# A fused MoE, attention and MoE kernel: the first group's turn and transfers in another order, four projection tiles behind the last mix, and a re-cut second routing

## The chip, the cores and the metric

The kernel runs on one core of one Trainium2 chip. The metric is the device time of one execution in microseconds, given as the median of several runs. All inputs and the output lie in HBM; one launch computes everything.

## The reference, cut to what matters

```python
# _moe_forward: E=8 experts, top 2 per token, capacity C=1280, h=256, F=512
x = x + 0.5 * ffn(layernorm(x))        # first routing and experts
x = x + attention(layernorm(x))        # 4 batches x 1024 tokens, 16 heads of 16
x = x + 0.5 * ffn(layernorm(x))        # second routing and experts
# attention: scores = Q K^T / 4 + lambda * (tanh(Q) J) tanh(K)^T, causal softmax,
#            out = probs V, then out Wo^T + bo
# ffn: probs = softmax(x Wg); two best experts; rows over the capacity dropped;
#      gelu(a) * g per expert; the two results added with normalised gates
```

## The kernel before, in words

4096 tokens of 256 values are kept as 32 tiles of 128 tokens. The program has three blocks, each ended by a barrier of all engines: first routing and experts; projections and attention; second routing and experts (`route` is called with `tail` only there).

**Start of attention.** Attention works on 16 groups, each of four heads of one batch. Before the scores of a group, every row's maximum is bounded by a pass of 48 products ("units", `max_unit` on TensorE, `seen` on VectorE). Then VectorE takes the maximum over the parts (`top_of`), TensorE turns it (`turn`), ScalarE negates it and its queue stores it as a further row of the queries (`negate`, `row`); the first score of the group waits for that row (`row_in`). The list `EVENTS` sets the order of units and turns, and TensorE, VectorE and ScalarE walk through the same list: before, each turn stands LAG = 4 units behind its group's last unit. The first 12 units of group 1 and the projections of the third half batch are mixed into this list ahead of the first scores (`first_events`). The banks for the products are lent out in the order of the list, so a unit waits until VectorE has read an earlier one.

The data of the first two halves come from `project`: `pack[0]` to `pack[3]` (high and low parts of queries and keys, 2 MB each) and the values. They go to HBM in `packs` and `values`, and come back as the tiles of a group (`load_queries_and_keys`, four transfers, 3 MB; `load_values`). The SP engine issues all of these from one queue, in program order. Group 0 gets its tiles directly. `pack[2]` and `pack[3]` hold other heads, which groups 2 and 3 need; `late_out` counts their arrival. The exponents (`wts`) are written to memory that a `pack` held.

**End of attention.** In the last group the output projection is computed tile by tile among the scores (`("o", t)`, one tile at each of 16 steps; `out_tile`, `add_out`), for tiles 0 to 15. The attended values of a half batch are divided by the softmax sums beforehand by GpSimd (`average`, two halves in each of the last three groups; `average_tail`). After the last mix, ScalarE stores the result, and the barrier follows.

**Second routing.** The other 16 tiles are projected in pairs (`pair`: eight matrix instructions, then `add_pair` and `pair_stats` on VectorE). The first pairs rest on data averaged in attention, the last four pairs on values that must first be divided (`average` in `route`): the reciprocals of the sums are regrouped by head by a DMA (`by_head`) and spread over the 16 rows of a head by a product with `spreader`. Statistics give variances and deviations for the tiles of one of `PARTS`; `normalize` makes the rows, by ScalarE for the groups of four tiles in `BY_ACT` and by VectorE for the others; then come `transposes` (TensorE), `turned` (copies on ScalarE), `logits`, `taken`, `turn_back`, and on VectorE the choice of experts, slots and lists, behind which the first gather of rows and the experts start.

## Time and profile before

| | us |
|---|---|
| median of 3 runs | 1552.32 (1543.54 to 1553.25) |
| the profiled execution | 1552.77 |
| its span, from the first to the last instruction | 1551.0 |
| mean TensorE clock granted in it | 0.957 of full speed |

The profile is one execution. Its span is divided into busy time of the engines; an idle time has the engine or transfer behind it that ended it. The blocks lie at 0 to 420 us (first routing and experts), 425 to 1121 us (projections and attention) and 1125 to 1551 us.

### The profile page before, as it was taken

Reading aid. Unit: us, or ns where it says so; the run is one execution under the profiler, and the core shown is the slowest. Engines: PE = TensorE matmul, PEld = TensorE weight load, DVE = VectorE, ACT = ScalarE, POOL = GpSimd, SP = SyncE. Lnnn points to the kernel's source line nnn. Section 1 sums busy time; section 2 is a strip of 40 time slices with the busy share of each in tenths; the row PEclk is TensorE's granted clock in tenths of the full one; section 3 lists DMA queues with packets and bytes.
Section 4 is the critical chain, followed back from the end, with each engine's and each line's share of the span. In section 5 each row is a group of like instructions: output and inputs, shape, how many; then the busy total and the mean of one; then the engine's idle time right before and its main releaser. Section 6 shows DMA issues by size and latency. Waiting matters only on the chain. (4 is left out here: it accounts for less than half of the span.)

```text
span 1551.0 us, 25160 instructions
## 1 busy us (share of the span) xinstructions
PE 1437.4 (93%) x8872; PEld 1091.9 (70%) x8874; DVE 994.4 (64%) x2526; ACT 719.2 (46%) x1106; POOL 681.1 (44%) x654
## 2 busy tenths in 40 slices
PE   4699999999878899999999999999896999999998
PEld 3589889899866555555555555555565998898998
DVE  7756655555368576777777677886367566565554
ACT  5333333333263455555556565665473333333332
POOL 1365565664435442323333332225303655656644
PEclk9799999999989698989999999999987999999999
DMA  9454433442299866665656569562073444335432
GB/s 306 139 105 100 94 64 87 102 93 38 29 194 273 263 185 157 168 174 134 178 149 178 131 177 258 170 188 97 30 236 116 105 98 97 60 92 103 94 38 26
DMA packets 125509, 206.48 MB, mean 133 GB/s; under 512 B 24280, under 2 KB 86232, under 8 KB 122520
## 3 DMA queue, kind: packets, MB, share of 16 engines
q1 hardware_dynamic: 89032, 157.96, 36.3%
q0 software_dynamic: 30720, 38.46, 15.1%
q10 hardware_dynamic: 5648, 8.66, 1.9%
q8 instruction: 62, 1.02, 0.3%
q14 instruction: 47, 0.39, 0.1%
HBM read 123.22 MB, written 82.54 MB: 133 GB/s over the span
## 5 line engine op out<-in xcount | busy, mean ns | idle before, releaser
L2188 ACT ACTIVATE a_wts<-a_s_psum 128x1024 f32<-128x1024 f32 (+1 forms) x384 | 301.7, 810 | 218.3 <-PE a_s_psum L2323 216.3
L2060 DVE CUSTOM_DVE_ANT_0 a_m_psum<-a_m_psum,mask 128x256 f32<-128x256 f32 (+2 forms) x492 | 248.4, 519 | 140.7 <-PE a_m_psum L2289 130.4
L2289 PE MATMUL a_m_psum<-a_kp,a_qp 96*128 96x512 f32 (+1 forms) x735 | 275.9, 403 | 26.1 <-DVE a_parts L2060 17.4
L2289 PEld LDWEIGHTS a_m_psum<-a_kp,a_qp 96*128 96x128 f32 x735 | 142.4, 196 | 159.5 <-DVE a_parts L2060 81.0
L1997 POOL TENSOR_SCALAR_AFFINE_SELECT a_wts<-a_wts 128x512 f32<-128x512 f32 x128 | 78.2, 634 | 329.0 <-ACT a_wts L2188 328.8
L1032 ACT ACTIVATE e_act_a<-e_a_psum 128x512 f32<-128x512 f32 (+1 forms) x192 | 101.2, 527 | 259.4 <-PE e_a_psum L1111 259.4
L2323 PE MATMUL a_s_psum<-a_qp,a_kp 97*128 97x512 f32 (+2 forms) x768 | 213.8, 361 | 0.7 <-DMA a_qp<-stats 0.4
L949 DVE TENSOR_TENSOR e_hid<-e_act_a,e_g_psum 128x512 f32<-128x512 f32 (+1 forms) x192 | 114.7, 597 | 141.5 <-PE e_g_psum L1111 136.8
L243 POOL DMA_INDIRECT e_slots<-normalized,e_token x160 | 166.2, 1039 | 81.7 <-issue 47.5
L1130 PE MATMUL e_o_psum<-e_w_hi,e_h_hi 128*128 128x256 f32 x640 | 183.4, 287 | 0.0
L890 POOL DMA_INDIRECT out<-e_res,e_sum_row x80 | 126.5, 1582 | 126.5 <-ACT e_res L1044 113.1
L890 POOL DMA_INDIRECT sums<-e_res,e_sum_row x80 | 126.5, 1581 | 126.1 <-ACT e_res L1044 104.9
L1130 PE MATMUL e_o_psum<-e_w_hi,e_h_lo 128*128 128x256 f32 x640 | 181.0, 283 | 0.0
L1130 PE MATMUL e_o_psum<-e_w_lo,e_h_hi 128*128 128x256 f32 x640 | 181.0, 283 | 0.0
L2063 DVE TENSOR_REDUCE a_parts<-a_m_psum 128x1 f32<-128x512 f32 x243 | 159.2, 655 | 10.5 <-PE a_m_psum L2289 7.0
L2339 PE MATMUL a_o_psum<-a_wts,a_vg 128*17 128x512 f32 (+3 forms) x1536 | 159.8, 505 | 4.0 <-POOL a_wts L1997 2.7
L2323 PEld LDWEIGHTS a_s_psum<-a_qp,a_kp 97*128 97x128 f32 x768 | 136.5, 195 | 19.0 <-ACT a_wts L2188 4.7
L1044 ACT ACTIVATE e_res<-e_o_psum,e_gate 128x256 f32<-128x256 f32 x160 | 75.9, 475 | 147.7 <-PE e_o_psum L1130 147.7
L1111 PE MATMUL e_a_psum<-e_s_hi,e_w_hi 128*128 128x512 f32 (+1 forms) x384 | 139.3, 363 | 5.4 <-DVE e_s_lo L929 2.8
L1111 PE MATMUL e_a_psum<-e_s_lo,e_w_hi 128*128 128x512 f32 (+1 forms) x384 | 136.0, 354 | 0.0
L1111 PE MATMUL e_a_psum<-e_s_hi,e_w_lo 128*128 128x512 f32 (+1 forms) x384 | 136.0, 354 | 0.0
L1111 PE MATMUL e_g_psum<-e_s_hi,e_w_hi 128*128 128x512 f32 (+1 forms) x384 | 135.9, 354 | 0.0
(292 smaller groups left out, 2702.9 us busy)
## 6 DMA issues: line engine op xcount, KB each, us to landing
packs<-x_res SPq DMA_DIRECT2D x48, 512.0 KB, 5.9
e_w_raw<-in_W_in SPq DMA_DIRECT2D x16, 1024.0 KB, 6.6
a_qp<-packs SPq DMA_DIRECT2D x15, 1024.0 KB, 8.0
a_kp<-packs SPq DMA_DIRECT2D x15, 1024.0 KB, 14.0
e_w_raw<-in_W_out SPq DMA_DIRECT2D x16, 512.0 KB, 8.4
normalized<-r_xn SPq DMA_DIRECT2D x16, 512.0 KB, 4.4
attended<-a_o_sb ACTq DMA_DIRECT2D x32, 256.0 KB, 4.6
a_qp<-packs SPq DMA_DIRECT2D x15, 512.0 KB, 10.1
```

The costliest lines, as they stand in the source:

```text
L243: pool.indirect_dma_start(held["slots"][e % 2][:, j * ROW:(j + 1) * ROW], None, xn_dram, bass.IndirectOffsetOnAxis(ap=held["token"][:, at: ...
L890: nc.gpsimd.indirect_dma_start(sum_dram, bass.IndirectOffsetOnAxis(ap=sum_row[:, at:at + 1], axis=0), res[j][:], None, bounds_check=last_r ...
L949: nc.vector.tensor_tensor(hid[q][:, 0:n], act_a[q][:, 0:n], g_ps[q][:, 0:n], ALU.mult).then_inc(hid_done, 1)
L1032: nc.scalar.activation(act_a[q][:, 0:n], a_ps[q][:, 0:n], ACT.Gelu).then_inc(gelu_done, 1)
L1111: last = nc.tensor.matmul(bank[q][:, 0:n], w_in_at(w, k, half + f), s[:, k, c0:c0 + n], start=(z == 0), stop=(z == len(terms) - 1))
L1130: last = nc.tensor.matmul(o_ps[(u * ST + c0 // P + j) % 2][:, 0:D], s[:, k, j * P:(j + 1) * P], w_out_at(w, k), start=(z == 0), stop=(z == ...
L2060: nc.vector.tensor_tensor_reduce(products, products, c["mask"][:, QC - width:], 1.0, MASKED, ALU.add, ALU.max, top).then_inc(max_read, 1)
L2063: nc.vector.reduce_max(top, products, AX.X).then_inc(max_read, 1)
L2188: nc.scalar.activation(wts[(u * NS + s) % 2][:, j, 0:w], s_ps[q % 2][:, 0:w], ACT.Exp).then_inc(weighed, 1)
L2289: nc.tensor.matmul(m_ps[bank((n, h, z))][:, 0:stream], qp[n % NB][0:PACK, h, qt * P:(qt + 1) * P], kp[n % NB][0:PACK, h, first * P:first * ...
L2323: last = nc.tensor.matmul(s_ps[q % 2][:, col - lead:col + w], kp[u][:, j, kt * P:(kt + 1) * P], qp[u][:, j, at - lead:at + w], start=True, ...
L2339: last = nc.tensor.matmul(o_ps[j * HP:j * HP + HV, q0:q0 + w], vg[u][:, kt, j, :], wts[(u * NS + s) % 2][:, j, col:col + w], start=(kt == ...
```

## The change

It has two places. **At the start of attention** the turn of group 0 stands right behind its 48 units. The load of group 1 is issued ahead of `pack[2]`; the values of group 1 count on the semaphore of group 0's values, so its units wait for the four loads of queries and keys alone; the load of the next half of x follows; then `pack[3]` is sent, SP waits until it has arrived, and then sends `pack[2]`. The first exponent waits for the arrival of `pack[3]`. **At the end of attention** four more tiles (16 to 19) are projected behind the last mix, ahead of the barrier (`AFTER_LAST`); their averages are made one group earlier. The second routing has six pairs instead of eight. The regrouping of the reciprocals is done by VectorE (`place`) and a product over 128 rows in place of a DMA. `PARTS` is cut at tiles 20 and 24, and ScalarE normalizes groups 0 to 4 in another order; it also blanks `lgT_ps`.

```diff
-IN_ATTENTION = TAIL - SEQ // P
+U_TILES = 4
+IN_ATTENTION = TAIL - U_TILES
...
-    PARTS = [slice(0, U), slice(U, NT)] if r == 0 else [slice(0, U), slice(U, U + U // 2), slice(U + U // 2, NT)]
+    PARTS = [slice(0, U), slice(U, NT)] if r == 0 else [slice(0, IN_ATTENTION), slice(IN_ATTENTION, TAIL), slice(TAIL, NT)]
...
-        BY_ACT = (1, 2, 3) if r == 0 else (0, 1, 2, 3, 4, 5)
+        BY_ACT = (1, 2, 3) if r == 0 else (0, 1, 2, 3, 4)
...
-                sp.wait_ge(inverted, 1)
-                sp.dma_start(by_head[:].rearrange("h (l c) -> h l c", c=PER_LANE),
-                             divisors[:]).then_inc(heads_in, 16)
...
+            def place(z):
+                half = slice(z * LANES // 2, (z + 1) * LANES // 2)
+                nc.vector.tensor_tensor(by_lane[:, half, :], divisors[:].unsqueeze(1).to_broadcast([P, LANES // 2, PER_LANE]),
+                                        on_lane[:, half].unsqueeze(2).to_broadcast([P, LANES // 2, PER_LANE]), ALU.mult).then_inc(placed, 1)
+
             if tail:
                 variances(0)
+                link(nc.vector.reduce_sum(on_lane[:], c["ident"][:].rearrange("p (h l) -> p l h", l=LANES), AX.X))
+                deviations(0)
                 dve.wait_ge(sums_in, 16)
                 nc.vector.reciprocal(divisors[:], divisors[:]).then_inc(inverted, 1)
-                deviations(0)
-                nc.vector.memset(lgT_ps[:], 0.0).then_inc(blank, 1)
+                dve.wait_ge(inverted, 1)
+                place(0)
+                place(1)
                 add_pair(0)
+                average(0)
                 add_pair(1)
+                average(1)
                 pair_stats(0)
-                average(0)
-                average(1)
                 pair_stats(1)
+                dve.wait_ge(stats_done, TAIL - IN_ATTENTION)
+                variances(1)
                 add_pair(2)
+                deviations(1)
                 add_pair(3)
...
+                normalize(5)
+                pair_stats(4)
                 add_pair(5)
...
             roots(0)
+            if tail:
+                nc.scalar.activation(lgT_ps[:], c["mask"][:], ACT.Copy, scale=0.0).then_inc(blank, 1)
...
+                pair(2)
+                transposes(0)
+                pair(3)
                 pe.wait_ge(averaged, 2)
-                transposes(0)
+                transposes(1)
+                pair(4)
                 pair(5)
-                pair(6)
-                transposes(1)
-                pair(7)
                 logits(0)
...
-            if k >= LAG and (k - LAG) % PER_GROUP == PER_GROUP - 1:
+            if k == PER_GROUP - 1:
+                EVENTS.append((0, GH - 1, None))
+            if k >= PER_GROUP + LAG and (k - LAG) % PER_GROUP == PER_GROUP - 1:
                 EVENTS.append(((k - LAG) // PER_GROUP, GH - 1, None))
...
+        IN_LAST = IN_ATTENTION - U_HALF
+        AFTER_LAST = [("o", t) for t in range(IN_LAST, IN_ATTENTION)]
...
             load_values(sp, tiles[0], v_dram, 0, loaded[0])
-            load_values(sp, tiles[1], v_dram, 1, loaded[1])
-            proj["last_packs"](sp)
+            load_values(sp, tiles[1], v_dram, 1, loaded[0])
             next_half(FIRST_LATER + 1)
+            proj["last_packs"](sp, FIRST_LATER + 1)
+            sp.wait_ge(proj["late_out"], 4 * 16)
+            proj["last_packs"](sp, FIRST_LATER)
             packs_out(FIRST_LATER, 0)
...
-                        if g >= GROUPS - 3:
-                            for z in range(2):
-                                average((g - GROUPS + 3) * 2 + z)
+                        for i in {GROUPS - 3: (0, 1), GROUPS - 2: (2, 3, 4, 5)}.get(g, ()):
+                            average(i)
...
-                if m == GROUPS * PER_GROUP - 1:
+                if m in (PER_GROUP - 1, GROUPS * PER_GROUP - 1):
                     top_of(n)
...
+                        if (g, q) == (0, 0):
+                            act.wait_ge(proj["late_out"], 4 * 16)
                         nc.scalar.activation(wts[(u * NS + s) % 2][:, j, 0:w], s_ps[q % 2][:, 0:w], ACT.Exp).then_inc(weighed, 1)
...
-                    pe.wait_ge(loaded[n % NB], (n // NB * NL + (NL if n % NB else 1)) * 16)
+                    pe.wait_ge(loaded[n % NB], (n // NB * NL + (2, NL - 1, NL)[n % NB]) * 16)
...
             groups(body)
+            ahead(AFTER_LAST)
```

**The SP queue at the start of attention.** Before (rows on `q_pack` are `pack[2]` and `pack[3]`, four transfers each; `a_qp`, `a_kp` are group 1's tiles and then group 2's):

```order
L1214 DMA values<-q_vals 128x272 x8
L1206 DMA packs<-q_pack 64x4x512 x4
L1250 DMA a_qp<-packs 64x4096
L1250 DMA a_qp<-packs 32x4096
L1250 DMA a_kp<-packs 32x4096
L1250 DMA a_kp<-packs 64x4096
L1256 DMA a_vg<-values 128x544 x2
L1206 DMA packs<-q_pack 64x4x512 x4
L1198 DMA x_res<-sums 128x4x256
L1206 DMA packs<-x_res 64x4x512 x4
```

After:

```order
L1218 DMA values<-q_vals 128x272 x8
L1254 DMA a_qp<-packs 64x4096
L1254 DMA a_qp<-packs 32x4096
L1254 DMA a_kp<-packs 32x4096
L1254 DMA a_kp<-packs 64x4096
L1260 DMA a_vg<-values 128x544 x2
L1202 DMA x_res<-sums 128x4x256
L1210 DMA packs<-q_pack 64x4x512 x8
L1210 DMA packs<-x_res 64x4x512 x4
L1218 DMA values<-q_vals 128x272 x4
```

Group 1's loads and the load of x moved ahead of both packs.

**TensorE at the end of attention and in the second routing.** Before (the branches are the barrier; `r_list_psum`, `r_lg_psum` and `r_tp_psum` from `p_wo` are pairs):

```order
L2339 MATMUL a_o_psum<-a_wts,a_vg 17x256 x4
L2436 UNCONDITIONAL_BRANCH
L2417 UNCONDITIONAL_BRANCH
L295 MATMUL r_list_psum<-p_wo,p_mean_third 128x256 x4
L295 MATMUL r_lg_psum<-p_wo,p_mean_third 128x256 x4
L761 MATMUL r_tp_psum<-r_by_head,r_spreader 128x512 x2
L295 MATMUL r_tp_psum<-p_wo,p_mean_third 128x256 x8
L295 MATMUL r_list_psum<-p_wo,p_mean 128x256 x4
L722 MATMUL r_tp_psum<-ident,r_xn 128x128 x8
L295 MATMUL r_lg_psum<-p_wo,p_mean 128x256 x4
L295 MATMUL r_tp_psum<-p_wo,p_mean 128x256 x4
L722 MATMUL r_tp_psum<-ident,r_xn 128x128 x8
```

After:

```order
L2346 MATMUL a_o_psum<-a_wts,a_vg 17x256 x4
L295 MATMUL a_m_psum<-p_wo,p_mean_third 128x256 x8
L2444 UNCONDITIONAL_BRANCH
L2425 UNCONDITIONAL_BRANCH
L295 MATMUL r_list_psum<-p_wo,p_mean_third 128x256 x4
L295 MATMUL r_lg_psum<-p_wo,p_mean_third 128x256 x4
L766 MATMUL r_tp_psum<-r_by_lane,r_spreader 128x512 x2
L295 MATMUL r_list_psum<-p_wo,p_mean 128x256 x4
L727 MATMUL r_tp_psum<-ident,r_xn 128x128 x8
L295 MATMUL r_lg_psum<-p_wo,p_mean 128x256 x4
L727 MATMUL r_tp_psum<-ident,r_xn 128x128 x8
L295 MATMUL r_list_psum<-p_wo,p_mean 128x256 x4
```

Four tiles (eight matrix rows into `a_m_psum`) stand ahead of the barrier, and behind the spreading product one pair instead of three stands ahead of the first transposes.

**ScalarE in the second routing.** Before (`r_rstd` are the roots, `r_xn` normalized tiles, `r_xnT` the copies of the turned rows):

```order
L625 ACTIVATE r_rstd<-r_tmp 128x16
L655 ACTIVATE r_xn<-x_res,r_shift,r_rstd 128x256 x16
L625 ACTIVATE r_rstd<-r_tmp 128x8
L631 COPY r_xnT<-r_tp_psum 128x1024
L655 ACTIVATE r_xn<-x_res,r_shift,r_rstd 128x256 x4
L631 COPY r_xnT<-r_tp_psum 128x1024
L655 ACTIVATE r_xn<-x_res,r_shift,r_rstd 128x256 x4
L625 ACTIVATE r_rstd<-r_tmp 128x8
L637 COPY r_lgT<-r_lgT_psum 104x512
L631 COPY r_xnT<-r_tp_psum 128x1024 x2
```

After:

```order
L628 ACTIVATE r_rstd<-r_tmp 128x20
L663 ACTIVATE r_lgT_psum<-mask 128x512
L658 ACTIVATE r_xn<-x_res,r_shift,r_rstd 128x256 x12
L628 ACTIVATE r_rstd<-r_tmp 128x4
L634 COPY r_xnT<-r_tp_psum 128x1024
L658 ACTIVATE r_xn<-x_res,r_shift,r_rstd 128x256 x4
L634 COPY r_xnT<-r_tp_psum 128x1024
L658 ACTIVATE r_xn<-x_res,r_shift,r_rstd 128x256 x4
L640 COPY r_lgT<-r_lgT_psum 104x512
L634 COPY r_xnT<-r_tp_psum 128x1024
L628 ACTIVATE r_rstd<-r_tmp 128x8
L634 COPY r_xnT<-r_tp_psum 128x1024
```

Group 3 is normalized behind the first copy, group 5 not at all here, and the third roots stand between two copies.

## Rows read from the trace of the kernel before

**Rows 1.** The page, part 1: busy time, share of the span and instructions of each engine.
```profile
PE 1437.4 (93%) x8872; PEld 1091.9 (70%) x8874; DVE 994.4 (64%) x2526; ACT 719.2 (46%) x1106; POOL 681.1 (44%) x654
```

**Rows 2.** Timeline of TensorE at the start of attention: start us, us, engine, line, operation.
```profile
504.99 0.58 PE L2289 MATMUL a_m_psum<-a_kp,a_qp 96*128 96x256 f32 x1 [3.99 <-DMA a_vg<-values]
...
507.07 0.40 PE L2295 MATMUL a_m_psum<-ident,a_tops 128*32 128x128 f32 x1 [0.54 <-DVE a_tops L2046]
...
513.87 1.33 PE L2323 MATMUL a_s_psum<-a_qp,a_kp 97*128 97x512 f32 x3 [0.43 <-DMA a_qp<-stats]
```

**Rows 3.** Timeline of VectorE there: the last product of the first group.
```profile
502.72 0.73 DVE L2060 CUSTOM_DVE_ANT_0 a_s_psum<-a_s_psum,mask 128x512 f32<-128x512 f32 x1
```

**Rows 4.** Timeline of ScalarE and its queue there.
```profile
507.80 0.61 ACTq L2126 DMA_DIRECT2D a_qp<-stats  x1
...
512.74 2.08 ACT L2177 ACTIVATE x_res<-x_res,q_shift,q_rstd 128x256 f32<-128x256 f32 x4 [2.95 <-DMA x_res<-sums]
...
515.24 1.02 ACT L2188 ACTIVATE a_wts<-a_s_psum 128x1024 f32<-128x1024 f32 x1 [0.42 <-PE a_s_psum L2323]
```

**Rows 5.** Timeline of the SP queue there.
```profile
477.50 6.72 SPq L1206 DMA_DIRECT2D packs<-q_pack  x4
...
484.62 2.96 SPq L1250 DMA_DIRECT2D a_qp<-packs  x2
...
490.67 9.56 SPq L1206 DMA_DIRECT2D packs<-q_pack  x4
...
500.27 1.67 SPq L1198 DMA_DIRECT2D x_res<-sums  x1
```

**Rows 6.** Timeline of GpSimd there and in the last group but one.
```profile
511.51 3.51 POOL L1986 MEMSET a_kp<- 1x4096 f32 x1 [14.11 <-issue]
...
523.28 1.81 POOL L1997 TENSOR_SCALAR_AFFINE_SELECT a_wts<-a_wts 128x512 f32<-128x512 f32 x3 [8.26 <-ACT a_wts L2188]
...
1078.44 1.81 POOL L1997 TENSOR_SCALAR_AFFINE_SELECT a_wts<-a_wts 128x512 f32<-128x512 f32 x3 [11.18 <-ACT a_wts L2188]
```

**Rows 7.** DMA issues: KB each, median us from issue to landing.
```profile
values<-q_vals SPq DMA_DIRECT2D x32, 136.0 KB, 1.9
```

**Rows 8.** Windows: busy us of each engine, then PEclk, DMA share, GB/s.
```profile
500.00:505.00 5.00, 0.91 (x3) 0.34 (x3) 3.51 (x11) 0.00 (x0) 0.00 (x0) 0.78 0.96 372
...
530.00:535.00 5.00, 5.00 (x28) 2.80 (x27) 1.13 (x4) 0.38 (x1) 3.14 (x4) 0.65 0.77 209
...
1120.00:1125.00 5.00, 0.74 (x8) 0.00 (x0) 0.00 (x0) 0.58 (x1) 0.00 (x0) 0.84 0.15 56
...
1125.00:1130.00 5.00, 4.62 (x11) 3.75 (x12) 3.15 (x13) 2.34 (x4) 2.28 (x8) 0.50 0.32 102
```

**Rows 9.** Timeline from attention's end to the second routing, all engines.
```profile
1121.43 0.33 ACTq L2136 DMA_DIRECT2D attended<-a_o_sb  x1
...
1125.38 3.75 PE L295 MATMUL r_list_psum<-p_wo,p_mean_third 128*128 128x256 f32 x8 [4.64 <-PEq L2436]
...
1145.90 1.04 PE L732 MATMUL r_lgT_psum<-r_xnT,wg 128*8 128x512 f32 x8
...
1148.33 0.21 ACT L625 ACTIVATE r_rstd<-r_tmp 128x8 f32<-128x8 f32 x1 [1.07 <-DVE r_tmp L193]
...
1148.91 1.93 ACT L631 COPY r_xnT<-r_tp_psum 128x1024 f32<-128x1024 f32 x2
```

**Rows 10.** The same timeline, further on.
```profile
1150.89 1.56 PE L732 MATMUL r_lgT_psum<-r_xnT,wg 128*8 128x512 f32 x8 [0.76 <-ACT r_xnT L631]
```

**Rows 11.** Groups of instructions, 1125 to 1153 us: busy us, mean ns, idle before.
```profile
L295 PE MATMUL r_tp_psum<-p_wo,p_mean 128*128 128x256 f32 x16 | 3.8, 379 | 0.0
...
L146 DVE BATCH_NORM_STATS2 stats<-x_res 128x6 f32<-128x256 f32 x16 | 5.8, 413 | 0.1
...
L456 DVE TENSOR_TENSOR x_res<-r_tp_psum,x_res 128x512 f32<-128x512 f32 x4 | 2.7, 687 | 2.3 <-PE r_tp_psum L295 2.3
...
L203 DVE SCALAR_TENSOR_TENSOR r_tmp<-r_tmp 128x8 f32<-128x8 f32 x2 | 0.3, 167 | 0.1
```

More of the change, by code:

```diff
@@ L350, in route @@
         if tail:
-            divisors, by_head = sb("divisors", [P, PER_LANE]), sb("by_head", [HEADS_K, KD * QC])
-            spreader = sb("spreader", [HEADS_K, P])
+            LANES = P // HEADS_K
+            divisors, by_lane, on_lane = sb("divisors", [P, PER_LANE]), sb("by_lane", [P, LANES, PER_LANE]), sb("on_lane", [P, LANES])
+            spreader = sb("spreader", [P, P])
+            y_at = [list_ps[:], lg_ps[1][:]]
             spread_ps = tp[0]
-            y_at = [list_ps[:], lg_ps[1][:]] + [tp[1][:, k, :] for k in range(KD)]
-            NY, PAIRS = len(y_at), SEQ // P // 2
-            PER_HALF = PAIRS // 2
-            assert NY == PAIRS
-            tp = [tp[0]] * 2 + [tp[0], tp[1]] * (G // 2 - 1)
-            sums_in, spreader_made, inverted, heads_in, spread, averaged, y_done, y_read = kit.sems("p", "sums_in spreader_made inverted heads_in spread averaged y_done y_read")
+            tp = [tp[(g + 1) % 2] for g in range(G)]
+            NY, PAIRS = len(y_at), (NT - IN_ATTENTION) // 2
+            PER_HALF = PAIRS // 3
+            sums_in, spreader_made, inverted, placed, spread, averaged, y_done, y_read = kit.sems("p", "sums_in spreader_made inverted placed spread averaged y_done y_read")
             o_in = kit.sems("p_o_in", "0 1")
@@ L674, in scalar @@
             else:
-                for g in range(G // CH):
-                    normalize(g)
+                normalize(0)
+                normalize(1)
+                normalize(2)
                 roots(1)
                 turned(0)
-                act.wait_ge(deviated, 2)
+                normalize(3)
+                turned(1)
                 normalize(4)
-                turned(1)
-                normalize(5)
-                roots(2)
                 taken(0)
                 turned(2)
+                roots(2)
                 turned(3)
@@ L744, in pair @@
             def pair(v):
-                half = v // PER_HALF - PER_HALF
-                mean_of = tail["mean_third"][v // PER_HALF] if half < 0 else tail["mean"][half]
+                half = v // PER_HALF - 1
+                mean_of = tail["mean"][half] if half >= 0 else tail["mean_third"][1]
                 if half >= 0:
@@ L758, in tensor @@
                 pe.wait_ge(spreader_made, 1)
-                pe.wait_ge(heads_in, 16)
                 for z in range(2):
-                    nc.tensor.matmul(spread_ps[:, z, :], spreader[:], by_head[:, z * QC:(z + 1) * QC], start=True, stop=True).then_inc(spread, 1)
-                for v in range(2, PAIRS + 1):
-                    pair(v)
+                    pe.wait_ge(placed, z + 1)
+                    nc.tensor.matmul(spread_ps[:, z, :], spreader[:], by_lane[:, z * LANES // 2:(z + 1) * LANES // 2, :].rearrange("p l c -> p (l c)"),
+                                     start=True, stop=True).then_inc(spread, 1)
+                pair(2)
+                transposes(0)
+                pair(3)
                 pe.wait_ge(averaged, 2)
-                transposes(0)
+                transposes(1)
+                pair(4)
                 pair(5)
-                pair(6)
-                transposes(1)
-                pair(7)
                 logits(0)
-                pe.wait_ge(y_read, 2 * PAIRS)
                 transposes(2)
@@ L1357, in sync @@
                             send_pack(sp, packs, pack[half], half, g, slice(0, K_HI), side_out, (1,))
-                else:
-                    sp.wait_ge(low_k, n + 1)
-                    sp.wait_ge(low_pool, 2 + n + 1)
-                    send_pack(sp, packs, pack[n], i, g, slice(K_HI, 8), late_out)
-                    sp.wait_ge(low_t, n + 1)
-                    send_pack(sp, packs, pack[n], i, g, slice(0, K_HI), late_out)
         def gpsimd(pool):
@@ L1639, in tensor, with last_packs @@
                 values(1, u)
-        def last_packs(sp):
-            i, g = STAGES[-1]
-            send_pack(sp, packs, pack[-1], i, g, slice(K_HI, 8), late_out)
-            send_pack(sp, packs, pack[-1], i, g, slice(0, K_HI), late_out)
-        proj["last_packs"], proj["values_out"], proj["side_out"] = last_packs, v_out, side_out
+        def last_packs(sp, n):
+            i, g = STAGES[n]
+            send_pack(sp, packs, pack[n], i, g, slice(K_HI, 8), late_out)
+            send_pack(sp, packs, pack[n], i, g, slice(0, K_HI), late_out)
+        proj["last_packs"], proj["values_out"], proj["side_out"], proj["late_out"] = last_packs, v_out, side_out, late_out
         functions = {"sync": sync, "gpsimd": gpsimd, "vector": vector, "scalar": scalar, "tensor": tensor}
@@ L1778, in attend @@
                 ORDER += events(g, q) + project_at(g, q)
+        ORDER += AFTER_LAST
         def kind(event):
@@ L2050, in seen @@
                 m = n * PER_GROUP + h * NU + z
-                if n and (h, z) == (0, 2):
+                if n > 1 and (h, z) == (0, 2):
                     top_of(n - 1)
@@ L2109, in vector @@
                         nc.vector.reciprocal(divisors, divisors).then_inc(inverted, 1)
+            step(AFTER_LAST)
             dve.wait_ge(stats_done, IN_ATTENTION)
@@ L2330, in mix @@
                 if (g, s) == (0, 0):
-                    pe.wait_ge(loaded[0], 16)
+                    pe.wait_ge(loaded[0], 2 * 16)
                 for kt, col, q0, w, lead in blocks:
```

16 lines of the change are left out of this document (4 added, 12 removed).

## The prediction

> **What bounds the kernel now.** I read the page's busy times first, then the timelines of TensorE at the two places that the diff touches, then what its idle times there ended with, and last the granted clock. TensorE is busy for 1437.4 us of 1551.0 [rows 1], so only its idle times and its slow stretches can be won back, and a change gains only what it takes out of that engine's own time line.
>
> The reader should see two holes. The first is at the start of attention: TensorE has nothing to do from 501.0 to 504.99 us, 3.99 us, and what ended it was the load of group 1, whose last part is the values [rows 2]. Later it waits 0.54 us for the maxima, and then 0.43 us for the row of the first group, which was issued at 507.80 and let the scores start at 513.87 [rows 2, 4]. Before that, however, VectorE is the slower of the two: its last maximum of group 0 runs to 503.45 us [rows 3], so even with the load there in time TensorE could hardly have turned group 0 before about 503.7. The clock granted to TensorE has a mean of 0.78 in 500 to 505 us and 0.65 in 530 to 535 [rows 8]: it went to the lower level (1.2 GHz) during the hole, and the upper one (2.4 GHz) came back only some 30 us later.
>
> The second hole lies between the blocks. TensorE's last mix ends at 1120.74 (1125.38 less 4.64 idle), ScalarE's store is issued at 1121.43, and the second routing starts at 1125.38 [rows 9]. It starts at half clock: 0.50 in 1125 to 1130 us, and the first pair takes 3.75 us where a pair at the full clock takes 1.9 (3.8 us for two) [rows 8, 9, 11].
>
> **The change at the start of attention.** SP issued `pack[2]` from 477.50, group 1's loads from 484.62, `pack[3]` from 490.67 (9.56 us for four issues, so its queue was full), and the load of x from 500.27 [rows 5]. With the loads in the first place they are issued some 6 to 7 us earlier, and their data have 2 MB less ahead of them, so they land well before 503. The 3.99 us wait for them goes. What is late next is VectorE's backlog: maximum until 503.45, then the reduction and the turn. I put the turn at 503.7 to 504.0, the next unit behind it at 503.9 to 504.2, against 504.99 now. That is 0.8 to 1.1 us, and the 0.54 us wait for the maxima on the way (it is now paid inside the hole) and the turn of 0.40 us itself leave the stretch behind it [rows 2]. What stands between the first unit of group 1 and the first score, 8.45 us now (504.99 to 513.44), becomes 7.5 to 7.9 us. The scores can start at 511.4 to 512.1, from 513.87, if their row is there. Its issue moves from 507.80 to about 504.4, and with the 6.1 us that it took (507.80 to 513.87) it lands at 510.5: in time. So the start gains 1.8 to 2.5 us.
>
> ScalarE must also be there. It waited 2.95 us for x and started the first exponent at 515.24 [rows 4]. The load of x now stands ahead of `pack[3]`, 14 us earlier, so this goes as well. The new wait of the first exponent is for `pack[3]`. Queued behind it on ScalarE are all exponents, and TensorE's third score waits for them. In the trace `pack[3]` took from 490.67 to about 511.5, when GpSimd's fill, which waits for both packs, began [rows 5, 6]: 20.8 us. The loads took SP from 484.62 to 490.67, 6.1 us, and the load of x 1.7 us [rows 5]; put at 477.50 they let `pack[3]` be issued from about 486 on. Behind the same loads it lands by 507, and the exponent comes at about 513. No cost, with 6 us in hand. `pack[2]` is issued only then and lands at about 513; GpSimd's fill of 3.51 us then ends at 517, before the first triangular cuts, at 523.28 now and at 521 then [rows 6]. Group 2's load stands behind all this as before and comes 0 to 3 us later; its units are called only in the last third of group 0. Nothing there reaches TensorE.
>
> SP's wait between the two packs leaves its queue empty for a moment: by the nearest row, 1.9 us from issue to landing of a small transfer [rows 7], about 2 us of transfer time lost in a stretch where the DMA share is near 1. It is covered by the same slack. The Trainium skill, "DMA: Bandwidth & Descriptors", section "Anatomy of one DMA", speaks against such a wait: it gives about 2.0 us fixed for each DMA whose completion is awaited, mostly the write receipt. The trace's 1.9 us agrees; by that page the term would be 2.0 us, and also nothing on TensorE.
>
> How much of the 1.8 to 2.5 us is left in the end depends on the clock, since it is won while TensorE runs at the lower level: if the upper level comes back at the same moment as before, only half of the lead is left, 1 us. If it comes back earlier, more, up to about 4 us. I take 2 us, with 0.5 and 4 as bounds.
>
> **The averages made one group earlier** lie behind the two that GpSimd already makes in the last group but one; it then sits idle for 11.18 us, up to the cuts at 1078.44 [rows 6]. They would have to take over 5.6 us each to be seen. I count them at nothing.
>
> **The tiles behind the last mix.** Four tiles are two pairs: 3.8 us at the full clock [rows 11]. They start at 1120.74. In 1120 to 1125 the mean clock is 0.84 [rows 8], so it is the upper level for most of it: they end at 1124.4 to 1125, and VectorE's last addition and statistics at 0.9 us later (0.41 for statistics, about as much for a tile's addition) [rows 11]. ScalarE's store takes perhaps 2.3 us from 1121.43, to 1123.7; the barrier then took some 1.5 us, up to 1125.19. Now VectorE comes last, at 1125.2, so the second routing starts at 1126.7, 1.3 to 1.6 us later than now.
>
> **The second routing.** From its start to the first logits TensorE needed 20.5 us (1125.38 to 1145.90) [rows 9]. Two pairs go, 3.8 us at the full clock. The DMA that regrouped the reciprocals goes; two multiplications of 128x512 and a small reduction come in its place on VectorE (two at 0.69, the nearest row, and one at up to 0.4), which lies behind the first two pairs. The spreading product itself stays. TensorE: pairs 0 and 1 mostly at the lower level again; they start 1.4 us later, but the upper level comes when it comes, so I put the end of both at most 0.4 us later than now. Behind them two pairs of 1.9 are missing: logits 3.4 us earlier, at 1142.5.
>
> But the second logits bind more. They began at 1150.89 behind two copies (1148.91, 1.93 us), which stood behind the roots at 1148.33, and these behind VectorE's variances [rows 9, 10]. VectorE's list, from the end of the first spreading product, some 7.5 us after the first pair's start now and at most 0.4 later then, so 1132.9, to the third variances: two averages and five additions at 0.69 (4.8), 12 statistics at 0.36 without their overlap (4.3), four normalized tiles of group 5, taken at the same 0.36 (1.4), 14 small ones at 0.17 plus 0.03 between them (2.8) [rows 11]. Sum 13.3 us, so 1146.2; the roots come at 1146.3, 2.0 us earlier. Only one copy of 1.0 us instead of two is left behind the roots, since the third stands ahead of them now: second logits at 1147.5, 3.4 us earlier. The two ways agree. Everything behind (copies, choice, lists, first gather) follows this chain, and the transfers of normalized rows are also issued earlier, so the experts start about 3.3 us earlier. Bounds: 1.5 us, if VectorE's new work is dearer or the barrier later; 5 us, if the clock rises sooner.
>
> **The sum.** 1552.77 (the profiled execution) less 2.0 less 3.3 is 1547.5; that execution lies 0.45 us above the median of the runs shown, so I say 1547.
>
> **The rivals.** *A tail that only moves.* If the four tiles run at the lower level (2 x 3.75 = 7.5 us), the barrier comes 5 us later and the second routing keeps less than 1 us of gain: 1552.3 - 2 - 1 = about 1549 to 1550. For it: the mean clock there is 0.84, not 1. Against: TensorE would then enter the routing warm. *The clock holds through the first hole.* With 2.7 us of idleness instead of 3.99, the lower level might last shorter. It lay over about 30 us in which TensorE was mostly busy but VectorE and ScalarE follow; worth 4 to 8 us more: 1539 to 1543. Against: 2.7 us idle is still long. *Late packs, slower than before.* The first exponent waits for `pack[3]`, and GpSimd's fill and with it every cut of group 0 for `pack[2]`. It decides if `pack[3]` lands after about 513, 6 us later than I think: then exponents wait, `pack[2]` lands past 522, the fill ends past 526, and the cuts are 3 us later than now and more, up to 8. Against the gain of 3.3 at the end: 1552 to 1557. For it: the queue's slow sends of 9.56 us for four [rows 5]. *Not what it says:* both gains are absorbed, by VectorE in attention and by the first gather: about 1552.
>
> The Trainium skill, "TensorE: Matmul & The Clock Gate", Part 1, says that the throttled state is the default and activity releases it, so four tiles in the second hole could give the routing the full clock from the start. That would be worth at most half of the first pair's 3.75 us [rows 9], 1.9 us more: 1545. The trace bears it out only in part, since the clock was low again at 1125 after a hole of 4.64 us, and a hole of 2 us stays.
>
> **How the numbers follow.** Forecast, both gains in their bounds (1544 to 1550): 0.52. Warm start of the routing, 1545: 0.10. Tail only moves, 1550: 0.12. Clock holds, 1541: 0.10. Late packs, 1555: 0.07. Absorbed, 1552: 0.09. The three runs shown differ by 9.7 us, 0.6%, without any change, so the range is 1539 to 1554. One per cent is 15.5 us, about what a measurement of this kernel can tell from no change: only the clock with more luck than I see would pass 1536.8, 0.05; only late packs at their worst would pass 1567.8, 0.02; within 1%: 0.93.
>
> **What the profile of after would show.** Right: no wait of TensorE for group 1's load, a turn at about 503.8, first scores near 511.7; roots of the third part about 2 us and second logits about 3.4 us earlier against the last mix; pairs 0 and 1 still mostly slow. Wrong: an exponent ended by `packs<-q_pack`, cuts of group 0 behind a fill, a barrier later than 1127, VectorE full without a gap from 1133 to 1150 with the variances past 1147.

## The result, and the profile after

| | before | after |
|---|---|---|
| median of the timed runs, us | 1546.49 (20 runs, 1537.91 to 1555.04) | 1540.92 (20 runs, 1533.98 to 1546.5) |
| ratio, 95% interval | | 0.9965 (0.995 to 0.9979) |
| the profiled execution: span, us | 1551.0 | 1542.8 |

The change gains 0.35%, 5.4 us of 1546.5 (3.2 to 7.7). The forecast was 5.3 us. Its absolute time, 1547, was set from three runs whose median was 1552.32; twenty runs put before at 1546.49.

**Start of attention after**, timeline of TensorE, ScalarE, SP and GpSimd (start, duration, in brackets the idle time and its releaser):

```profile
501.25 0.49 PE L2296 MATMUL a_s_psum<-a_kp,a_qp 96*128 96x512 f32 x1
504.57 0.39 PE L2302 MATMUL a_m_psum<-ident,a_tops 128*32 128x128 f32 x1 [2.82 <-DVE a_tops L2050]
...
511.51 0.75 PE L2330 MATMUL a_s_psum<-a_qp,a_kp 97*128 97x512 f32 x3
...
512.30 1.02 ACT L2195 ACTIVATE a_wts<-a_s_psum 128x1024 f32<-128x1024 f32 x1 [1.82 <-PE a_s_psum L2330]
...
484.33 24.95 SPq L1210 DMA_DIRECT2D packs<-q_pack  x8
...
513.99 3.51 POOL L1991 MEMSET a_kp<- 1x4096 f32 x1 [15.83 <-issue]
519.72 1.82 POOL L2002 TENSOR_SCALAR_AFFINE_SELECT a_wts<-a_wts 128x512 f32<-128x512 f32 x3 [2.23 <-ACT a_wts L2195]
```

The wait for group 1's load [rows 2] is gone; what is left of the hole, 2.82 us, ends with VectorE's maxima. The scores wait for no row. The first exponent waits for TensorE, not for `packs<-q_pack`, and comes at 512.30, not 515.24 [rows 4]. GpSimd's fill and first cuts lie early, as forecast.

**The clock** in the same stretch, windows (busy time of PE, PEld, DVE, ACT, POOL, then the granted clock, DMA share, GB/s):

```profile
500.00:505.00 5.00, 2.02 (x6) 0.99 (x6) 4.48 (x15) 0.00 (x0) 0.00 (x0) 0.68 0.53 197
505.00:510.00 5.00, 4.24 (x13) 3.11 (x12) 4.11 (x14) 2.44 (x6) 0.00 (x0) 0.64 0.98 247
...
520.00:525.00 5.00, 4.67 (x15) 1.73 (x14) 3.84 (x12) 1.44 (x4) 4.85 (x8) 0.50 0.78 212
...
530.00:535.00 5.00, 4.78 (x21) 3.03 (x19) 2.92 (x9) 3.35 (x5) 1.68 (x2) 1.00 0.96 269
```

It falls to the lower level as before, comes back twice for some 3 us (hence the 0.64), and is back for good at about 529 us, where before stood at 0.65 in 530 to 535 [rows 8].

**End of attention and second routing after**, timeline:

```profile
1113.55 2.75 PE L2346 MATMUL a_o_psum<-a_wts,a_vg 128*17 128x128 f32 x24
...
1116.24 3.72 PE L295 MATMUL a_m_psum<-p_wo,p_mean_third 128*128 128x256 f32 x16
...
1120.45 0.43 DVE L146 BATCH_NORM_STATS2 stats<-x_res 128x6 f32<-128x256 f32 x1
1121.46 1.28 ACT L628 ACT_TABLE_LOAD   x1 [4.49 <-PEq L2444]
...
1121.65 1.96 PE L295 MATMUL r_list_psum<-p_wo,p_mean_third 128*128 128x256 f32 x8 [1.69 <-PEq L2444]
...
1123.45 1.89 PE L295 MATMUL r_lg_psum<-p_wo,p_mean_third 128*128 128x256 f32 x8
...
1125.05 1.29 DVE L469 TENSOR_TENSOR r_by_lane<-r_divisors,r_on_lane 128x512 f32<-128x512 f32 x2
1125.89 1.52 PE L766 MATMUL r_tp_psum<-r_by_lane,r_spreader 128*128 128x512 f32 x3 [0.54 <-DVE r_by_lane L469]
...
1136.62 1.04 PE L737 MATMUL r_lgT_psum<-r_xnT,wg 128*8 128x512 f32 x8
...
1141.03 1.04 PE L737 MATMUL r_lgT_psum<-r_xnT,wg 128*8 128x512 f32 x8 [0.67 <-ACT r_xnT L634]
...
1147.23 3.44 PE L727 MATMUL r_tp_psum<-ident,r_xn 128*128 128x128 f32 x16
...
1149.23 1.01 ACT L634 COPY r_xnT<-r_tp_psum 128x1024 f32<-128x1024 f32 x1 [1.30 <-PE r_tp_psum L727]
...
1158.97 1.11 PE L804 MATMUL r_list_psum<-ones_bf,r_hot_bf 128*64 128x1 bf16 x8 [3.69 <-DVE r_hot_bf L535]
```

The last mix ends at 1116.30 (1113.55 + 2.75). The four tiles take 3.72 us at the full clock, VectorE's last statistics end at 1120.88, and the barrier opens 0.6 us later. The hole before the first pair is now 1.69 us, not 4.64 [rows 9], and both first pairs run at the full clock. Counted from the end of the last mix, the first logits come at 20.3 us (before 25.2), the second at 24.7 (30.15) [rows 9, 10], the count of choices at 42.7 (46.4), the first gather at 56.7 (60.5). Of the 5.4 us won at the second logits 1.7 are lost again by the count. One set of transposes, 1.97 us long at the full clock, falls into a stretch of the lower clock in both kernels. In after it takes 3.44 us, one step later than in before, and ScalarE's copy waits 1.30 us for it. In before it is this one, and no copy waits for it:

```profile
1152.39 3.07 PE L722 MATMUL r_tp_psum<-ident,r_xn 128*128 128x128 f32 x16
```

The last mix itself came 4.4 us earlier than in the profile of before. That is not all the change's, as the experiments show.

### The profile page after: what moved, and what is told of

It reads as the page before. It is cut to its first block and busy times, and to the rows that moved or that the text cites. A ratio compares the mean times of both kernels' runs of the same rounds, so it can differ in the third digit from the quotient of the medians.

```text
span 1542.8 us, 25167 instructions
## 1 busy us (share of the span) xinstructions
PE 1432.7 (93%) x8874; PEld 1089.0 (71%) x8874; DVE 997.9 (65%) x2534; ACT 717.9 (47%) x1103; POOL 682.8 (44%) x654
## 5 line engine op out<-in xcount | busy, mean ns | idle before, releaser
L2067 DVE TENSOR_REDUCE a_parts<-a_m_psum 128x1 f32<-128x384 f32 (+1 forms) x244 | 159.7, 654 | 10.3 <-PE a_m_psum L2296 6.8
## 6 DMA issues: line engine op xcount, KB each, us to landing
a_kp<-packs SPq DMA_DIRECT2D x15, 1024.0 KB, 13.9
```

The costliest lines, as they stand in the source:

```text
L2067: nc.vector.reduce_max(top, products, AX.X).then_inc(max_read, 1)
```

## The experiments

Two marks are used for every kernel. **The tail** is the time from the end of the last mix to the end of the last instruction. It is nearly the same in the profiles of one ending (within 1.0 us for the old one, 0.7 for the new one), and what differs between kernels lies in its first 55 us: from the count of choices to the end it is 382.3 us in every profile below but one (381.9). **The mark of group 1** is the start of VectorE's maximum over the parts of that group, some 39 us behind the first scores.

### The four parts apart

The start alone is before with all edits of the start; the end alone is the rest of the diff. The transfers alone leave the turn of group 0 where it was; the turn alone is this:

```diff
+            if k == PER_GROUP - 1:
+                EVENTS.append((0, GH - 1, None))
+            if k >= PER_GROUP + LAG and (k - LAG) % PER_GROUP == PER_GROUP - 1:
```

**Start alone.** 

> The kernel before with the whole part at the start of attention and nothing of the end. If the two parts add and each does what its rows say: first exponent about 2.9 us earlier than before (as in the profile of after), last mix 2.9 to 4.4 us earlier, second routing as before; 0.997 to 0.9985 of the time before. If the start's lead is only the clock's luck in one profiled execution: within 1 us of before. If the lead of 4.4 us at the last mix came from the averages made one group earlier and not from the start: last mix less than 3 us earlier here.

**End alone.** 

> The kernel before with the four tiles behind the last mix and the re-cut second routing, start of attention as before. If the second routing starts warm because the hole behind the last mix is short: pairs 0 and 1 at 1.9 us each, logits near 20.3 us behind the last mix (25.2 before), hot count 42.6 behind it (46.4 before), so 3 to 4 us faster, 0.9975 or so. If the tail only moves: 0 to 1 us. Last mix at the same place as before, within 1 us, unless the earlier averages matter.

**Transfers alone.** 

> The kernel before with the new order of transfers (and the wait of the first exponent), but the turn of group 0 still four units behind its last unit. If the wait for group 1's load is what holds the start: that wait goes, units of group 1 run on at 501 to 503, the turn waits for the maxima at about 503.7, and the first exponent is 1.5 to 2.9 us earlier, most of the whole. If the place of the turn matters, less than 1.5 us here.

**Turn alone.** 

> The kernel before with the turn of group 0 right behind its units, transfers as before. The turn comes at 503.8 and the row about 1.5 us after it is stored, but the units of group 1 still wait for their load until about 505 and the first exponent for x; so the first scores come at most 0.9 us earlier (the 0.43 us wait for the row and the turn's 0.40 us), the first exponent 0 to 0.5 us. If the row was what bound the start, 2 us.

| kernel | ratio to before (95%) | tail, us | mark of group 1 |
|---|---|---|---|
| before | | 428.72 | 552.96 |
| start alone | 0.9997 (0.9976 to 1.0019) | 428.57 | 550.39 |
| end alone | 0.996 (0.9941 to 0.9978) | 424.95 | 550.27 |
| transfers alone | 0.9998 (0.9978 to 1.0018) | 427.76 | 548.22 |
| turn alone | 0.9993 (0.9968 to 1.0017) | 427.72 | 550.80 |
| after | 0.9965 (0.995 to 0.9979) | 424.92 | 548.83 |

The timed runs show a gain for the end alone, 6.2 us (3.4 to 9.1), and none for the start, 0.5 us (-2.9 to 3.7), which leaves room for the 2 us forecast. The old ending has a tail of 428.2 us (mean of five profiles, 427.7 to 428.7), the new one of 424.6 (four, 424.3 to 424.95), three of these nine from runs further down: 3.6 us. The start alone cannot be told from nothing, so the ratio expected of it (0.997 to 0.9985) was missed. Its first exponent came at 513.97, 1.3 us earlier than before and not 2.9. The last mix of the end alone came 10.5 us earlier than in before, where 1 us at most was expected: the place of the last mix in one execution says little. The turn's place shows no gain either: by itself it lets the scores start at 513.00, and ScalarE still waits 3.50 us for x. In the transfers alone the turn comes behind four units of group 1, and the first scores are no later than in after:

```profile
504.38 0.40 PE L2293 MATMUL a_m_psum<-ident,a_tops 128*32 128x128 f32 x1 [1.46 <-DVE a_tops L2042]
...
510.55 1.16 PE L2321 MATMUL a_s_psum<-a_qp,a_kp 97*128 97x512 f32 x3
```

The end alone, with the start of before, also has an early mark of group 1, 550.27. Its clock came back at about 519.5 us in that execution (low once more from 526.7 to 529.6) and not at 533. So a lead of 2.7 us there can be had without any change, and no single pair of profiles can size the start.

### What the end is made of

Placing the reciprocals can be undone in after (the DMA and the product over 16 rows again) or put alone into before. In the same way the first pairs can be made to start warm without moving a tile, by products of the identity behind the last mix:

```diff
             groups(body)
+            run(32)
```

**32 products in before.** 

> The kernel before with 32 products of the identity with itself (no result is used) behind the last mix, about 3.7 us at the full clock, which fill the hole between the blocks; nothing else is changed. If the end's gain is largely a warm start: the second routing starts at the same place, pairs 0 and 1 take 1.9 us each instead of 3.75 and less, logits 2 to 3 us earlier against the last mix (from 25.2), and the kernel is 2 to 3 us faster, 0.998 or 0.9985. If the gain comes from the two pairs that left the routing: pairs may be quicker, but VectorE or the clock behind them takes it back, within 1 us of before.

**After with the DMA back.** 

> The kernel after with the reciprocals regrouped by a DMA and spread by a product over 16 rows, as before, in place of VectorE's two multiplications and reduction. The reciprocals are there about 3 us behind the start of the routing, and the DMA takes some 2 us; the spreading product then starts at the same place as in after or up to 1 us later, and VectorE has 1.8 us less to do. Forecast: within 1 us of after, 0.9965 of before. If the DMA was what the re-cut routing gained from: logits 1 us later or more, 0.997 to 0.998.

**Placing alone in before.** 

> The kernel before with one part of its second routing changed: the reciprocals are placed by VectorE (one reduction, two multiplications) and spread by a product over 128 rows, in place of the DMA. The two first pairs run at the lower clock as before and end 10 us behind the last mix; with the DMA the spreading product starts at 10.9 there. If the DMA is what the re-cut routing got rid of, as the run with the DMA back says: spreading product 1 us earlier, hot count about 1 us earlier against the last mix (from 45.5 to 46.4), 0.999 to 1.0 of before. If placing alone is the whole gain of the end: hot count at 43, 0.9975.

**16 products in before.** 

> The kernel before with 16 products of the identity (no result is used) behind the last mix. In the run with 32 each product showed as two rows and the 64 took 7.4 us, 3.1 us too many; 16 take 3.6 us and fit the hole. If a warm start is worth something by itself: hot count 1 to 2 us earlier than in before (46.4 behind the last mix, or 42.0 behind the routing's start), 0.999. If TensorE then only waits for the DMA, 2.6 us as in the run with 32, and loses its clock there: hot count 42 to 44.6 behind the routing's start, 1.000 to 1.002 of before.

**Placing and 16 products in before.** 

> Both: the kernel before with VectorE's placing and with the 16 products behind the last mix; no tile is moved and no list re-cut. If warm start and placing pay only together, and moving the tiles is just another way to stay warm: spreading product 4.4 us behind the routing's start (6.5 before), hot count 43 to 44 behind the last mix, 0.998. If the two pairs taken out are needed for the gain: hot count later than 45, 0.9995 to 1.0.

| kernel | ratio to before (95%) | tail, us | first pair | spreading product | first logits | count |
|---|---|---|---|---|---|---|
| before | | 428.72 | 4.64 | 10.94 | 25.16 | 46.41 |
| placing alone | 0.9998 (0.998 to 1.0015) | 426.16 | 3.39 | 8.61 | 22.53 | 43.86 |
| 16 products | 1.0014 (0.9994 to 1.0033) | 431.26 | 4.36 | 10.82 | 26.70 | 48.94 |
| placing, 16 products | 0.9993 (0.9973 to 1.0014) | 427.76 | 4.33 | 8.52 | 22.52 | 45.49 |
| 32 products | 1.0053 (1.003 to 1.0077) | 434.65 | 7.90 | 14.20 | 30.08 | 52.34 |
| after, DMA back | 0.997 (0.995 to 0.9991) | 427.71 | 5.71 | 11.68 | 24.10 | 45.77 |
| after | 0.9965 (0.995 to 0.9979) | 424.92 | 5.35 | 9.59 | 20.32 | 42.67 |

The last four columns are us behind the end of the last mix. The 16 products, timeline of TensorE:

```profile
1115.27 3.84 PE L1268 MATMUL a_s_psum<-ident 128*128 128x128 f32 x32
1119.70 1.97 PE L295 MATMUL r_list_psum<-p_wo,p_mean_third 128*128 128x256 f32 x8 [0.59 <-PEq L2437]
1121.50 1.89 PE L295 MATMUL r_lg_psum<-p_wo,p_mean_third 128*128 128x256 f32 x8
1126.16 1.95 PE L761 MATMUL r_tp_psum<-r_by_head,r_spreader 8*128 8x512 f32 x4 [2.77 <-DMA r_by_head<-r_divisors]
1128.04 5.41 PE L295 MATMUL r_tp_psum<-p_wo,p_mean_third 128*128 128x256 f32 x16
```

Here the first two pairs start at the full clock, as in after, and nothing is saved by it: TensorE then waits 2.77 us for the regrouping DMA, which the slow pairs had hidden, and the low clock comes now, so that the next two pairs take 5.41 us. Where the placing is alone the first two start cold and the next two take 3.62 us, about as in before (3.72):

```profile
1116.65 3.30 PE L295 MATMUL r_list_psum<-p_wo,p_mean_third 128*128 128x256 f32 x8 [3.39 <-PEq L2444]
1119.75 2.28 PE L295 MATMUL r_lg_psum<-p_wo,p_mean_third 128*128 128x256 f32 x8
1121.87 1.88 PE L768 MATMUL r_tp_psum<-r_by_lane,r_spreader 128*128 128x512 f32 x4
1123.58 3.62 PE L295 MATMUL r_tp_psum<-p_wo,p_mean_third 128*128 128x256 f32 x16
```

**Stretch by stretch**, after against the profile of before: the first pair starts 0.7 us later behind the last mix (5.35 for 4.64). From there to the spreading product it is 4.2 us instead of 6.3. From the spreading product to the first logits it is 10.7 us instead of 14.2, and this is the same in all four profiles of the new ending and within 0.03 us in all five of the old one: it is the two pairs that left the routing. The second logits follow 0.6 us sooner, and 1.7 us are lost up to the count. That makes the 3.8 us between these two tails.

**Placing alone** has a tail of 426.2, 2.0 us under the mean of the old ending, but little of that is shown to be the placing's. First, its hole before the first pair is 3.4 us. So it is in three of the five old endings, with a mean tail of 427.9. In the other two, before and the start alone, the barrier opened 3.6 to 3.8 us behind ScalarE's store and not 2.5. Second, its spreading product came 5.2 us behind the first pair, against 6.3 to 6.6 in four of the five, which have no wait for the DMA:

```profile
1128.93 2.82 PE L295 MATMUL r_lg_psum<-p_wo,p_mean_third 128*128 128x256 f32 x8
1131.68 1.98 PE L761 MATMUL r_tp_psum<-r_by_head,r_spreader 8*128 8x512 f32 x4
```

These are before's. The gain is in the two pairs ahead of the product, which the placing does not touch: the clock came back 3.9 us behind the start of the first pair, in those four 5.4 to 6.0. The fifth old ending (24 products in the start alone, below) had it back after 3.1 us, and there the DMA does show:

```profile
1123.44 3.50 PE L295 MATMUL r_list_psum<-p_wo,p_mean_third 128*128 128x256 f32 x8 [3.42 <-PEq L2440]
1126.78 1.89 PE L295 MATMUL r_lg_psum<-p_wo,p_mean_third 128*128 128x256 f32 x8
1129.38 1.95 PE L761 MATMUL r_tp_psum<-r_by_head,r_spreader 8*128 8x512 f32 x4 [0.71 <-DMA r_by_head<-r_divisors]
```

So in before's order the placing takes out a wait of 0 or 0.7 us, as the clock falls, and from the product to the first logits it is 13.9 us instead of 14.2. That is 1 us at most. Its timed ratio, 0.9998, fits its first theory, 0.999 to 1.0. Its count at 43.9 looks like the second, the whole gain, but that lead is mostly the clock's.

**With the 16 products as well** the count is at 45.5. That is the case "later than 45" of its expectation, by which the two pairs taken out are needed for the gain. This run is no clean test of a warm start, since the products outlast the hole and the first pair starts 0.9 us later than with the placing alone. The spreading product and the first and second logits come at the same places in the two, and the 1.6 us between their tails are lost behind the second logits.

**The tiles and the new lists with the DMA** have a tail of 427.7, inside the scatter of the old ending. VectorE's list stops 3.11 us at the first average:

```profile
1133.69 0.69 DVE L468 TENSOR_TENSOR p_mean<-p_mean,r_tp_psum 128x512 f32<-128x512 f32 x1 [3.11 <-PE r_tp_psum L760]
```

TensorE waits 2.28 us for the DMA, and the pair behind the wait runs at the lower clock:

```profile
1132.56 1.95 PE L760 MATMUL r_tp_psum<-r_by_head,r_spreader 8*128 8x512 f32 x4 [2.28 <-DMA r_by_head<-r_divisors]
1134.44 3.04 PE L295 MATMUL r_list_psum<-p_wo,p_mean 128*128 128x256 f32 x8
```

That kernel's expectation, within 1 us of after, fell by its profile: the first logits are 3.8 us later and the tail 2.8 us longer, as its rival said and more. Part of that is the order of after's list, which puts the average ahead of the second addition; the runs do not separate it. The timed runs do not show this loss: its ratio of 0.997 is nearly after's, and like the others in this table it has an interval of some 0.2% to each side, too wide for 2 us.

By the profiles, then, either part alone gives 1 us at most and both together 3.6 us: the tiles shorten the routing and warm it, and the placing takes out the wait that would eat this. It rests on one profile of each of the mixed kernels.

That the 32 products cost 8.2 us by the runs (6.5 by the tail) was my mistake of size: each shows as two rows of 0.12 us, so they took 7.4 us and the first pair came 3.3 us later than in before; the rest is the wait of 2.61 us and the clock behind it, as with 16.

### Holding the clock through the first hole

24 products (24, then 11) ahead of the turn of group 0 in after, and 24 in the start alone:

```diff
             def turn(n, h):
+                if n == 0:
+                    pe.wait_ge(blank, 1)
+                    for _ in range(24):
+                        nc.tensor.matmul(o_ps[0:HV, 0:P], c["ident"][:, 0:HV], c["ident"][:], start=True, stop=True)
                 pe.wait_ge(topped, n + 1)
```

**24 in after.** 

> The kernel after with 24 products of the identity (no result is used, about 2.8 us at the full clock) ahead of the turn of group 0, so that TensorE is busy through the hole of 2.82 us there. If that hole is what lowers the clock: granted clock near 1 from 501 to 511 us, first exponent 1.5 to 3 us earlier than in after, and 3 to 6 us faster than after, 0.993 to 0.9945 of before. If the clock falls anyway (by the idle times behind it, when TensorE waits for VectorE at 509 to 522, or otherwise): low again before 520, within 1.5 us of after.

**24 in the start alone.** 

> The kernel before with the part at the start of attention alone, as in the first experiment, and the same 24 products ahead of the turn. The two theories as for the kernel after: if the hole is what lowers the clock, 3 to 6 us faster than the start part alone, so 0.996 to 0.998 of before; if it falls anyway, within 1.5 us of before, like the start part alone.

**11 in after.** 

> The kernel after with 11 products of the identity ahead of group 0's turn; the 24 of the run before took 5.3 us (48 rows), so 11 take 2.4 us, inside the hole, and the turn is not late. If the low clock of 500 to 530 us comes from this hole: clock 1 up to 520 at least, first exponent 1 to 2 us earlier than in after, and 2 to 4 us faster than after. If it falls anyway, as in the run with 24 (1.00 up to 510 us, then 0.5 to 0.84 up to 530): within 1.5 us of after, 0.9965 of before.

Measured: 0.9984 (0.9961 to 1.0008), 1.0009 (0.9986 to 1.0032) and 0.9944 (0.9922 to 0.9965, 6 runs). The 24 took 5.4 us and made the turn late, and the first ratio is above after's, though the intervals overlap; the clock held up to 510 us and stood at 0.50 in 520 to 525. The 11 took 3.59 us, not the 2.4 expected, and the turn came 1.0 us behind the maxima. The windows of that run are:

```profile
500.00:505.00 5.00, 4.95 (x23) 3.12 (x23) 4.47 (x15) 0.00 (x0) 0.00 (x0) 0.66 0.49 185
505.00:510.00 5.00, 3.57 (x20) 2.33 (x17) 3.83 (x14) 2.92 (x6) 0.00 (x0) 1.00 0.96 238
510.00:515.00 5.00, 4.69 (x16) 3.75 (x17) 3.83 (x13) 1.02 (x1) 0.93 (x1) 0.59 1.01 333
515.00:520.00 5.00, 4.18 (x13) 3.17 (x13) 2.83 (x8) 2.80 (x4) 2.58 (x1) 0.50 0.93 294
520.00:525.00 5.00, 4.57 (x14) 2.89 (x12) 4.03 (x11) 2.37 (x5) 3.94 (x6) 0.50 1.00 256
```

Here the clock fell at about 500.7 us, while TensorE still ran the units and 1.3 us before the products began, and was back at about 504. It is full in 505 to 510 us, where after has 0.64, and falls all the same behind it, where TensorE waits for VectorE's maxima. The mark of group 1 is at 549.22, no earlier than in after (548.83). So the low clock of this stretch is not the hole's alone, in this run and in the one with 24, and the theory that it is falls. The ratio of 0.9944 is lower than after's, but the intervals overlap, and the profile shows no gain at the place that was changed. I don't count it as a better version; nothing here is shown to beat after.

## Where the start's lead went

The mark of group 1 lies at 551.3 us on average in the seven kernels with the old transfers (550.3 to 553.0) and at 549.5 in the four with the new ones and no added products (548.2 to 550.7): 1.7 us, close to the 2 us forecast. Behind it, one interval from mark to mark is 39.40 us when nothing disturbs it, in any kernel. But the intervals 2 to 3, 4 to 5, 6 to 7 and 8 to 9 are in some executions 1.1, 2.1 or 3.3 us longer. Before and the end alone have the same code there. This is the interval 2 to 3 in windows, first of before:

```profile
605.00:610.00 5.00, 4.57 (x15) 3.14 (x14) 3.91 (x11) 2.27 (x4) 1.81 (x3) 0.52 1.03 260
610.00:615.00 5.00, 5.00 (x17) 2.54 (x16) 1.43 (x6) 1.54 (x3) 0.00 (x0) 0.50 0.91 266
```

The same stretch in windows of the end alone:

```profile
605.00:610.00 5.00, 4.27 (x21) 2.50 (x22) 2.94 (x10) 1.84 (x4) 0.83 (x2) 1.00 0.97 228
610.00:615.00 5.00, 4.83 (x35) 3.07 (x34) 2.90 (x9) 3.09 (x5) 3.08 (x5) 1.00 0.45 184
```

The clock went down for about 10 us in the one and not in the other. Before and the turn alone have the same ending and spans 10.8 us apart, of which 7.7 lie between marks 1 and 10. That the timed runs spread for the same reason is likely, but they have no marks. From mark 1 to mark 10 the seven kernels with the old transfers take 358.6 us on average (356.8 to 364.7) and the seven with the new ones 362.6 (356.9 to 364.8). The interval 2 to 3 was 3.3 us longer in six of the seven new and two of the seven old. So the start's 1.7 us may well be given back by clock that is lost more often behind it. With seven draws of each that is likely, not shown, and why the new order should lose it more often stays open: in the interval 2 to 3 TensorE waits 1.34 us for VectorE in before and in the end alone alike.

## Why the prediction was right

The time was right (5.4 us of gain, 5.3 forecast), and so was the end as a sum: 3.3 forecast, 3.6 measured by the tail. That the times agree within 0.1 us is luck, since the measured gain is only known as 3.2 to 7.7 us, and by the timed runs alone nearly all of it is the end's. Point by point:

- **Wait for group 1's load: right.** It is gone, the turn waits for VectorE, the exponent has no pack to wait for, and the cuts no fill. The first exponent came at 512.3 where 513 was forecast, and the transfers alone did it; the turn's place, which I had given a share, adds nothing that shows. The turn came at 504.57 and not 503.8, since VectorE's maxima were late. The Trainium skill, "DMA: Bandwidth & Descriptors", section "Anatomy of one DMA", is about transfers that GpSimd issues, and SP issues these; the prediction's 1.9 us [rows 7] is this trace's own.
- **2 us "left in the end": not shown in the time.** At group 1 the lead is 1.7 us. The step that failed to carry is "how much of the 1.8 to 2.5 us is left in the end depends on the clock": I looked for that only up to 535 us, and the start alone measures 0.9997. The rival "absorbed" may hold for this part, but by the clock in groups 2 to 9 and not by VectorE; that is likely, not shown.
- **The tiles behind the last mix: right in size**, 3.72 us at the full clock. The barrier opened 0.6 us behind VectorE, not 1.5. The rival of a tail that only moves fell.
- **"Pairs 0 and 1 mostly at the lower level again": wrong.** They ran at 1.96 and 1.89 us. This was the rival of the warm start. The Trainium skill, "TensorE: Matmul & The Clock Gate", Part 1, says that activity releases the throttle, and the trace agrees: with the tiles in the hole both pairs ran at the full clock. The way from the first pair to the spreading product became 2.1 us shorter. It shows at the first logits, 4.8 us earlier where the sum said 3.4, and no longer at the end, since 1.7 us are lost behind the second logits. Warmed by themselves, the same pairs made the tail 3.1 us longer with the DMA and 1.6 longer with the placing.
- **The two missing pairs: right.** From the spreading product to the first logits it is 3.5 us less; 3.4 forecast.
- **The DMA against VectorE's placing: right for before's order, wrong for after's.** I took it as an even exchange behind two pairs. In before the spreading product came 6.3 us behind the first pair (10.94 - 4.64) with no wait of TensorE for it, since the slow pairs covered the DMA. Once the pairs are quick, waits of 2.28, 2.61 and 2.77 us appear, and with the DMA back in after the tail is 2.8 us longer. The sum put this term and the warm start at nothing; measured, each needs the other.
- **Second logits 3.4 us earlier: 5.4**, of which the clock and the copies behind it took 1.7 back; the third roots came at 23.6 us behind the last mix, not 25.6. First gather 3.7 us earlier, 3.3 forecast.

## What to carry to other kernels

A slow stretch can hide a wait: before a step is made quicker, work out what the next engine would wait for if it were, and remove that first. Before a gain is given to a part, look whether it begins at that part: placing alone was ahead before its own instructions mattered, by the clock. Keeping TensorE busy with empty products moved its low clock to the next wait in these runs and gained nothing. And where an execution's own spread (here 12 to 17 us) exceeds the gain, measure a change between two marks that bracket it in several profiles, and see by the timed runs whether the lead reaches the end.

## What the hardware showed unexpectedly

A float32 product of 128x128 shows as two rows (16 products, 32 rows, 3.84 us), twice the cost that I had taken from counting instructions. And the same code, at the same step of the same interval, ran at a granted clock of 0.50 in one execution and 1.00 in another, for 10 us. The barrier, too, opened 2.5 us behind ScalarE's last store in four executions of the old end of attention and 3.6 to 3.8 us behind it in two.
